# Sorted rows stay in SBUF as the experts' sums, and the extra items move behind the first 24 tiles

## The reference, cut to what matters

```
x = x + gnn(layernorm(x), edges)              # 6250 rows of 256; one edge per row counts
tokens = layernorm(x)
probs = softmax(tokens @ router_w.T);  rw, re = top_k(probs, 2);  rw = rw / rw.sum()
out = tokens
for e in range(8):
    h = gelu(tokens @ w1[e] + b1[e]);  y = h @ w2[e] + b2[e]
    out = out + combine[:, e] * y             # combine is 0 but for the row's two experts
x = x + out
```

## Time and profile before

| | us |
|---|---|
| time, median of 3 runs | 503.22 (495.93 to 503.9) |
| the profiled execution's own time | 506.39 |
| its span | 504.6 |
| PE, DVE, ACT, POOL busy in the span | 382.1, 342.0, 276.1, 244.4 |
| mean granted TensorE clock | 0.907 |

### The profile page before, as it was taken

One profiled execution on the slowest core, in us unless ns is written; L12 is line 12 of the kernel. 1 busy time (PEld: TensorE's weight loads), 2 busy tenths in 40 slices (PEclk: granted clock), 3 DMA queues, 4 the chain that ended last, 5 costly groups with the idle time before them and its releaser, 6 DMA issues.

```text
span 504.6 us, 11001 instructions
## 1 busy us (share of the span) xinstructions
PE 382.1 (76%) x3546; PEld 334.2 (66%) x3546; DVE 342.0 (68%) x1160; ACT 276.1 (55%) x715; POOL 244.4 (48%) x241
## 2 busy tenths in 40 slices
PE   3597874898978782645883999798787787889991
PEld 2486764887868672534772988687576676769990
DVE  2549595597979888793662768576465655668871
ACT  3157542455454645752642577476564656569870
POOL 8468884475757510005465445545445354533332
PEclk9998987997979887756996899989999999999996
DMA  4263535374646443222233222212212122121110
GB/s 151 64 164 117 173 111 161 114 202 145 202 139 199 146 119 94 76 78 58 64 87 87 68 76 67 75 56 68 73 47 73 54 66 66 54 66 43 45 54 19
DMA packets 30085, 48.21 MB, mean 96 GB/s; under 512 B 5720, under 2 KB 22898, under 8 KB 30028
## 3 DMA queue, kind: packets, MB, share of 16 engines
q0 software_dynamic: 10896, 29.61, 20.0%
q1 hardware_dynamic: 18378, 17.32, 11.7%
q10 hardware_dynamic: 756, 0.58, 0.4%
HBM read 34.42 MB, written 13.07 MB: 94 GB/s over the span
## 4 chain that ended last, share of the span: by engine, by line
PE 38%; issue 14%; another core or an unknown queue 13%; ACT 13%; DVE 11%; POOL 5%; DMA 2%; DVEq 1%; ACTq 0%; POOLq 0%
PE bank L1490 9%; PE bank L1299 8%; PE bank L1512 7%; PE bank L1302 3%; POOL out_dram L560 3%; ACT h L732 3%; PE bank L1290 3%; PE bank L1323 2%; PE bank L1428 2%; DVE h_lo L1225 2%; PE bank L1505 2%; DVE acc L1243 1%; ACT acc L613 1%; ACT work L720 1%
## 5 line engine op out<-in xcount | busy, mean ns | idle before, releaser
L512 POOL DMA_INDIRECT acc<-in_x_dram,index x98 | 114.8, 1171 | 57.9 <-ACT work L603 30.9
L732 ACT ACTIVATE h<-bank,b_col 128x128 f32<-128x128 f32 x250 | 78.1, 365 | 85.2 <-PE bank L1490 58.1
L551 POOL DMA_INDIRECT work<-token_table,order x76 | 75.0, 987 | 98.0 <-DVE order L1175 52.5
L1490 PE MATMUL bank<-work,w_hi 128*128 128x128 f16 x1000 | 103.4, 223 | 20.1 <-issue 17.2
L1243 DVE SCALAR_TENSOR_TENSOR acc<-bank,work,acc 128x256 f32<-128x256 f32 (+1 forms) x125 | 60.4, 483 | 77.8 <-remote 41.8
L1490 PEld LDWEIGHTS bank<-work,w_hi 128*128 (+1 forms) x1000 | 83.5, 100 | 25.9 <-issue 20.0
L1490 PE MATMUL bank<-work,w_lo 128*128 128x128 f16 x500 | 93.8, 223 | 2.5 <-issue 2.5
L560 POOL DMA_INDIRECT out_dram<-acc,order x49 | 48.9, 998 | 95.2 <-DVE acc L1243 90.3
L1299 PE MATMUL bank<-w_ext,work 128*128 128x260 f32 x196 | 62.0, 445 | 14.7 <-ACT work L596 7.2
L1512 PE MATMUL bank<-w_hi,h_lo 128*128 (+1 forms) x250 | 69.0, 276 | 1.7 <-issue 1.7
L1512 PE MATMUL bank<-w_lo,h_hi 128*128 (+1 forms) x250 | 69.0, 276 | 0.9 <-issue 0.9
(11 more groups left out here) (210 smaller groups left out, 712.0 us busy)
## 6 DMA issues: line engine op xcount, KB each, us to landing
acc<-in_x_dram SPq DMA_DIRECT2D x42, 112.0 KB
work<-in_L_ffn_w_dram SPq DMA_DIRECT2D x16, 256.0 KB
token_table<-row_out SPq DMA_DIRECT2D x28, 133.0 KB
token_table<-row_out SPq DMA_DIRECT2D x3, 931.0 KB
acc<-in_x_dram,index POOLq DMA_INDIRECT x98
work<-token_table,order POOLq DMA_INDIRECT x76
acc<-in_x_dram SPq DMA_DIRECT2D x1, 784.0 KB
out_dram<-acc,order POOLq DMA_INDIRECT x49
```

Of the source, the lines that this page charges most:

```text
L512: nc.gpsimd.indirect_dma_start(out=xds[:, t % RING, n, :], out_offset=None, in_=x, in_offset=bass.IndirectOffsetOnAxis(ap=index[:, n, t:t ...
L551: nc.gpsimd.indirect_dma_start(out=rows[:, k % ROWS_RING, :], out_offset=None, in_=table, in_offset=bass.IndirectOffsetOnAxis(ap=order[:, ...
L732: last = nc.scalar.activation(h32[:, i % RINGS, f * P:(f + 1) * P], bank[i % RINGS][:, f * P:(f + 1) * P], ACT.Gelu, bias=bias_of(f), scal ...
L1490: last = nc.tensor.matmul(bank[i % RINGS][:, f * P:(f + 1) * P], first_weights(i, lo, c, f), x2T[:, r, half, c * P:(c + 1) * P], start=(m ...
```

## The change

The array for the sums becomes `rows`: 50 slots of a whole row. The gather of tile k writes its slot, and the rest is added there in place. No tile is gathered twice, and nothing is cleared.

- 49 gathers instead of 76. They no longer wait for any accumulation: gather k waits only for gather k - 16 to have landed. All 49 stand ahead of the first scatter in POOL's queue, and the 49 scatters follow; the first 24 tiles are complete only when the last extra is.
- 49 preps instead of 76, one with each of the items 0 to 46 (two stand ahead). All transposed halves `x2T` stay in SBUF.
- Items: the two of the tiles 0 to 23 (48 items), the 27 extras, the two of the tiles 24 to 48 (50 items).
- An extra's tile is now named by a register on PE too (its `x2T` columns) and on DVE (its row's weight and its sum).
- Every fourth tile is normalised by DVE, the others by ACT. One addition for a tile instead of two.
- The experts' words are loaded in two parts (6 words ahead of the first item, 7 before item 75), and 7 words with the extras' tiles before item 48 on PE and DVE.
- Six small DVE instructions of the cuts move from among the marks to behind the copy of `order`; the product that made the extras' columns of `order` goes.
- `row_out` moves into the work array. The four clears go.

```diff
-ITEMS = [(k, None) for k in range(EXTRAS)] + [(EXTRAS + q, n) for q in range(TILES) for n in range(2)]
+AHEAD = 24
+ITEMS = ([(q, n) for q in range(AHEAD) for n in range(2)] + [(k, None) for k in range(EXTRAS)]
+         + [(q, n) for q in range(AHEAD, TILES) for n in range(2)])
+READY = 2
+TURN = 4
...
+        def prep_of(i):
+            return i + READY if i + READY < TILES else None
+        def done(q):
+            return SUMS[LAST_EXTRA if q < AHEAD else EXTRAS + 2 * q + 1]
...
             def gather_rows(k):
-                column = TILES + k if k < EXTRAS else k - EXTRAS
-                if k >= ROWS_RING:
-                    pool.wait_ge(s_acc, SUMS[last_item(k - ROWS_RING)])
-                elif k >= FIRST_ROWS:
-                    pool.wait_ge(s_acc, SUMS[last_item(k - FIRST_ROWS)])
+                at_least(pool, s_rows[k % ROWS_RING], 16 * (k // ROWS_RING))
                 nc.gpsimd.indirect_dma_start(
-                    out=rows[:, k % ROWS_RING, :], out_offset=None, in_=table,
+                    out=rows[:, k, :], out_offset=None, in_=table,
...
-            for k in range(PREPS):
+            for k in range(TILES):
                 gather_rows(k)
-                if k - SCATTER_LAG >= EXTRAS:
-                    scatter(k - SCATTER_LAG - EXTRAS)
-            for q in range(TILES - SCATTER_LAG, TILES):
+            for q in range(TILES):
                 scatter(q)
...
                 hidden_lo(i)
-                if n != 1:
...
+                if prep_of(i) is not None:
+                    sorted_lo(i + READY)
+                    add_normal(i + READY)
+                if i + 4 < TILES and by_vector(i + 4):
+                    turn_normal(i + 4)
+                if i == FIRST_EXTRA:
+                    load_tiles()
+                if i == LAST_EXTRA:
+                    load_experts(FIRST_WORDS, WORDS)
...
+            def sorted_columns(i, half, c):
+                k, n = ITEMS[i]
+                if n is None:
+                    return x2T[:, bass.ds(tiles[k], 1), half, c * P:(c + 1) * P].rearrange("p t d -> p (t d)")
+                return x2T[:, k, half, c * P:(c + 1) * P]
```

More of the change, by code:

```diff
@@ L1457, in walked, with extra @@
                 return 0 <= i < len(ITEMS) and ITEMS[i][1] is not None
+            def extra(i):
+                return 0 <= i < len(ITEMS) and ITEMS[i][1] is None
             def first_addresses(i, f, c):
@@ L1463, in first_addresses @@
                         address(first_weights(i, lo, c, f), True)
+                if extra(i) and f == 0:
+                    for half in range(2):
+                        address(sorted_columns(i, half, c), False)
             def second_addresses(i):
@@ L1514, in second, with load_experts @@
                 last.then_inc(s_y, 1)
-            experts = {}
-            def load_experts():
+            experts, tiles = {}, {}
+            def load_experts(begin, end):
                 _, words = nc.values_load_multi_w_load_instructions(
-                    expert_of[0:1, :], engines=[ENG.PE], min_val=0, max_val=64 ** PACK - 1,
+                    expert_of[0:1, begin:end], engines=[ENG.PE], min_val=0, max_val=64 ** PACK - 1,
                     skip_runtime_bounds_check_because="sums of the steps of a walk over the pairs are experts")
-                for q in range(TILES):
-                    word, at = words[q // PACK], 6 * (q % PACK)
+                for q in range(begin * PACK, min(end * PACK, TILES)):
+                    word, at = words[q // PACK - begin], 6 * (q % PACK)
@@ L1524, in load_experts, with load_tiles @@
                     experts[q] = [(word, at), (word, at + 3)]
+            def load_tiles():
+                pe.wait_ge(s_extra, 1)
+                _, words = nc.values_load_multi_w_load_instructions(
+                    extra_tile[0:1, :], engines=[ENG.PE], min_val=0, max_val=64 ** PACK - 1,
+                    skip_runtime_bounds_check_because="tiles' numbers, or the dummy's, as the cuts give them")
+                for k in range(EXTRAS):
+                    tiles[k] = words[k // PACK], 6 * (k % PACK)
@@ new lines, in _ @@
+            load_experts(0, FIRST_WORDS)
+            for step in range(2):
+                unpack(0, step)
+            for f in range(KT):
+                for c in range(KT):
+                    first_addresses(0, f, c)
+            for k in range(READY):
+                sorted_transpose(k)
+            for i in range(len(ITEMS)):
+                if i == FIRST_EXTRA - 2:
+                    load_tiles()
+                if i == LAST_EXTRA - 1:
+                    load_experts(FIRST_WORDS, WORDS)
+                first_item(i)
+                if prep_of(i) is not None:
+                    sorted_transpose(i + READY)
```

295 lines of the change are left out of this document (140 added, 155 removed).

## The result

| | before | after |
|---|---|---|
| median, us | 501.55 (495.93 to 503.9, 4 runs) | 543.34 (542.23 to 547.12, 4 runs) |
| ratio | | 1.0887 (1.0769 to 1.1005) |
| profiled execution, its span | 506.39, 504.6 | 542.23, 540.4 |
| busy: PE, DVE, ACT, POOL | 382.1, 342.0, 276.1, 244.4 | 372.0, 312.4, 259.1, 211.4 |

A forecast was written before the change was run, and what follows sets the result against it. PE bounds the experts' part, losing time beside POOL's back-to-back DMAs. Span: 504.6 - 6.2 - 0.5 + 1.0 - 57.0 + 40 + 12 = 493.9; likeliest time 493 us, range 461 to 521, the forecast's own 480 to 507.

The forecast's parts named there:

- loss beside the gathers' run: First items, beside 49 gathers at 1.25 us: PE was to lose 40 us, bounds 18 and 60.
- loss beside the scatters' run: Last 50 items, beside 24 ready scatters at 1.29 us and later ones: PE was to lose 12 us.
- DVE and ACT in the first 48 items: Items with a prep: DVE's and ACT's load was to fit under PE's 1.66 us, costed at 0, bound 7.
- the tail: End of the kernel: to stay as it is, since POOL would be through before the end.
- the first item's start: PE's first item in the experts' part: to begin at 237, within 1.5.
- the two shares: Fractions of time PE loses beside POOL's runs: 0.68 for the gathers, 0.25 for the scatters.
- rival 2: Gathers' run stops PE almost wholly, 47 and 5 behind, scatters 29: time about 521; chance 0.20.
- my upper bound of 29: Scatters' run: loss at a share of 0.68, 24 us, with 4.6 behind it.
- the 6.2 us of 27 preps: Experts' part: 27 preps less at 0.23 us each on PE, -6.2 us.
- Registers: Loads of 6, 7 and 7 words in place of one of 13: +1.0 us in all.
- the loss of 58 us: Experts' part of the kernel before: 58.2 of 254.4 us lost, taken to go with POOL's DMAs back to back.
- rival 3: POOL's new bursts cost nothing, the holes having another cause that goes with the old order: time 440; chance 0.05.

The follow-up runs named there:

- set 1: First four follow-ups: the changed kernel with gathers, scatters or both spaced by waits, or POOL fills behind gathers; the kernel before took 501.5 us there.
- e9: The changed kernel itself again, where the kernel before takes 422.61 us; 427.32 us, ratio 1.011.
- e16: e3's kernel plus eight unread gathers of 64-byte rows and eight of 1064-byte rows, where the kernel before takes 493.22 us; 480.19 us.
- e15: Kernel before with a POOL fill of 224 columns behind each gather and all scatters, unfilled, behind the last gather; 504.05 us.
- e1: Changed kernel with gather k, from 5 on, waiting until tile k - 5 is prepared, scatters as they were; 496.44 us.
- e3: Changed kernel with waits that space both runs: gathers one for each prepared tile, scatters one for each item; 476.59 us, ratio 0.9519.
- e8: e3's kernel with ACT's normal rows an item earlier, where the kernel before takes 423.05 us; 422.04 us, ratio 0.9978.
- e11: Kernel before with a POOL fill of 224 columns behind each gather and behind the scatters between gathers; 422.72 us.
- e17: The changed kernel a third time, where the kernel before takes 492.76 us; 540.08 us, ratio 1.0983.
- e10: e3's kernel again, where the kernel before takes 422.61 us; 426.25 us, ratio 1.0087.
- e6: e3's kernel plus eight unread gathers of 64-byte rows and eight of 1064-byte rows, where the kernel before takes 423.05 us; 424.01 us.

## Why the prediction was wrong

The forecast's sum gave a span of 493.9, and 540.4 was measured. By its own terms:

| term | forecast | measured | difference |
|---|---|---|---|
| loss beside the gathers' run | 40 | 58 | +18 |
| loss beside the scatters' run | 12 | 33 | +21 |
| DVE and ACT in the first 48 items | 0 | 8 | +8 |
| the tail | as it is | 5.0 longer | +5 |
| the first item's start | 237.3 | 231.5 | -5.8 |

Together 493.9 + 46 = 540. The last row is no gain of the change: in the four kernels of set 1, whose first parts are alike, the first item starts anywhere from 230.8 to 238.2. How the measured ones come out: from item 0 to item 47 the kernel after takes 144.2 us, and 86.4 in e9's pace, so 58; from item 77 to 124 it takes 101.2, and 68.2 at 1.45, so 33; 47 items at 1.84 less 1.66 are 8.

**The step that failed** is the two shares. I had a run of 12 gathers in which PE lost 0.68 of the time, and carried the share to a run of 49. But three items were done beside it, which fits a stop that takes a while to set in: in e16 PE goes on in its stride until the fourth gather, at 330.6. The right reading of the earlier trace rows was the 6.68 us in which PE did nothing, as rival 2 had it. Of the 55.6 us from PE's first item to the end of the last gather (231.5 to 287.1) 47.6 were lost, a share of 0.86, and nearly all of what lay past the onset. The second term of the same sum failed as well: behind the run I had 4.6 us, and the stop went on for 9.4 us and then the low clock, some 10 of loss. For the scatters I halved a share (0.50 to 0.25, a loss of 12) that belonged to pairs of DMAs with 3.68 us of rest behind them, and 33 were lost. 24 ready scatters are a long run like the other, e15 does three items in 44 us beside its own, and the time is above even my upper bound of 29. Rival 2 was the nearest, with 521: it had the loss beside the first run right, at 47, took 5 behind it, and 29 for the second. In the chances, same and slower add up to 0.31 and 0.23 by their own terms, not to 0.30 and 0.24.

**What held.** That PE bounds the part and POOL's unspaced DMAs are the loss: in e1 to e3 each trough goes with its own run's spacing, and e15 takes the old loss from items 47 to 77 by leaving no scatter between the gathers. The 30 items without a prep stand at 1.43, so the 6.2 us of 27 preps were earned. Registers cost 0.8 at item 77 (2.2 for 1.43).

**DVE and ACT.** I counted DVE's load (1.57 of 1.66) and ACT's, and both fit. It wasn't the load but the order in ACT's queue: the normal rows of tile i+3 stand behind item i's other work, and three of four of them are ACT's. They were some 0.3 us late for the transposes of about every other item; e8 shows it by moving them an item ahead, which brought 0.08 us an item and left DVE's turn late.

**The tail.** "The tail stays as it is" was argued from POOL being through with its backlog. It was, and yet 5 us came on behind the last landing, in every run of the changed kernel on either kind of chip (15.0), and none in the kernel before (9.9 to 10.0). It is POOL's closing drain: 8.9 us in every form with the change's 196 indirect DMAs, whatever the chip and the spacing, and 3.82 in the kernel before. 16 gathers more gave 6.60 (12.8 in all), 27 more 7.50 (13.7) in either place, before with its scatters last 5.29 (11.5). What sets the drain's length stays open.

**What no row of before could show** is that the loss of 58 us on which the whole sum stood comes with the chip or the occasion, and not with the kernel alone. In two of the six sets (the first result counted as one) the kernel before takes 423 us, its items stand at 1.70 and 1.53 (e11), and rival 3, bursts that cost nothing, is simply true: the change then costs 1.1%. Its price of 440 was too high because the loss isn't in this part alone: in the traces the first item starts at 206.5 to 210.1 there, and at 226.8 to 238.2 on the others.

The Trainium skill, SBUF — State Buffer, "Who interferes with whom", has PE and ACT wait on nobody. e9 agrees (25 items in 44 us beside a run of gathers), the first result and e17 don't (two in 56). Since 64-byte rows stop PE like wide ones, it may be right of the ports and silent on the path that counts.

## What to carry to other kernels

Don't take DMAs of POOL off a natural pace for nothing: one that only waits for its data runs as fast as POOL can issue, and on a chip that stops, nearly each further microsecond of such a run is a microsecond of PE. A wait for an engine's progress costs nothing where nothing stops (e10 against e9) and brought 12% of the changed kernel where it does (476.6 for 543.3, in two sets in which the kernel before took 501.5). When a share of loss is read from a short run, take its onset and its steady part apart before you carry it to a long one. And time a kernel on more than one chip before its losses are put down to its code.

## What the hardware showed unexpectedly

The same kernel takes 423 us in two sets and 493 to 502 in four (the first result's among them), within 1 to 2% in each. The two kinds differ in who gives way. On the free chip (e6) the probe's gathers stretch to 1.13 us and fall into the items' step of 1.43; on the stopping one (e16) they keep 0.94 and 1.25 apart, and PE stops:

```profile
303.62 1.13 POOL L601 DMA_INDIRECT half_sum<-token_table,order  x1 [0.30 <-issue]
305.06 1.12 POOL L601 DMA_INDIRECT message<-token_table,order  x1 [0.30 <-issue]
```

```profile
329.39 0.94 POOL L601 DMA_INDIRECT half_sum<-token_table,order  x1 [0.30 <-issue]
330.64 0.95 POOL L601 DMA_INDIRECT message<-token_table,order  x1 [0.30 <-issue]
```

The distance that matters is narrow. On a chip that stops, a long run at 1.25 stops PE; a run of 14 gathers at 1.42 still costs 13.7 us (e15); scatters with one for each item hold the items at 1.71 for 1.43 (e3); gathers with one for each item cost nothing (e3 does 37 items at 1.85 beside them, a free chip 1.84, and the earlier trace rows has them 1.66 apart without a loss).
